# Expert stage of a graph and transformer block: tokens routed in two parts of 13 and 12 groups in place of three of 10, 9 and 6

## What is computed

```python
xn = _layernorm(x, axis=-1)
x = x + gnn(xn, edge_attr_64, src, dst, ...) + mix(xn, ...)   # edge attention; linear attention and MLP
x = x + ffn(_layernorm(x, axis=-1), ...)

# ffn: six experts of three 256x256 layers, two chosen per token
rh = relu(features @ router_w1 + router_b1)
expert_logits = softmax(rh @ router_w2 + router_b2)
top_w, top_i = top_k(expert_logits, 2)
routing_weights = softmax(top_w)
# h1, h2, expert_out of each expert; the two chosen outputs, weighted and added
```

## Time and profile before

| | |
|---|---|
| median of three runs | 2500.79 us |
| the profiled execution's own time | 2505.82 us |
| its span | 2504.1 us |
| TensorE busy | 1926.2 us (77%) |
| GpSimd busy | 1668.5 us (67%) |
| VectorE busy | 1556.8 us (62%) |
| ScalarE busy | 611.9 us (24%) |
| mean granted TensorE clock | 0.859 of full speed |

### The profile page before, as it was taken

How to read it: one execution, slowest core, us unless ns; L and a number is a source line. 1 busy time by engine, 2 the same in 40 slices (tenths; PEclk the granted TensorE clock), 3 DMA queues, 4 the chain that set the end, 5 groups by cost and what they waited for, 6 DMA issues and landing times.

```text
span 2504.1 us, 39252 instructions
## 1 busy us (share of the span) xinstructions
PE 1926.2 (77%) x11133; PEld 1530.7 (61%) x11133; DVE 1556.8 (62%) x3687; ACT 611.9 (24%) x2634; POOL 1668.5 (67%) x1278
## 2 busy tenths in 40 slices
PE   3899577659887777777878767878775778999992
PEld 1444476547766665665666656656654667888882
DVE  4778599877766565566566655656654883226263
ACT  1333388611111111111111111111101323433430
POOL 5554466688888888888888888888884277316164
PEclk8999756569988898898888888888887888999996
DMA  5766788534454444445544444455456455437363
GB/s 155 205 205 189 253 299 294 190 98 133 124 151 127 123 128 123 123 124 134 140 127 123 127 123 123 123 146 132 123 125 182 133 163 153 129 111 199 102 191 96
DMA packets 310586, 378.65 MB, mean 151 GB/s; under 512 B 119740, under 2 KB 263832, under 8 KB 307376
## 3 DMA queue, kind: packets, MB, share of 16 engines
q1 hardware_dynamic: 168932, 234.02, 30.1%
q0 software_dynamic: 141568, 143.66, 23.3%
HBM read 291.57 MB, written 84.76 MB: 150 GB/s over the span
## 4 chain that ended last, share of the span: by engine, by line
PE 34%; POOL 19%; DVE 9%; issue 8%; DMA 5%; ACT 2%; DVEq 2%; SPq 0%; ACTq 0%; POOLq 0%
PE bank L692 32%; POOL wexp L633 17%; DMA wexp<-xn_rows,a_src 4%; PE bank L1018 1%; POOL g_all L679 1%; DVEq L1508 1%; DVE work L1744 1%; DVE work L1749 1%; DVE st L1752 1%; DVE onehot L1668 1%; DVE acc L1680 1%; DVE acc L1766 1%; DVE work L1518 0%; DVE work L1526 0%; SPq L339 0%
## 5 line engine op out<-in xcount | busy, mean ns | idle before, releaser
L633 POOL DMA_INDIRECT wexp<-xn_rows,a_src x900 | 1126.8, 1252 | 274.0 <-issue 258.4
L692 PE MATMUL bank<-wexp,onehot 125*125 125x257 f32 x1800 | 548.7, 459 | 269.9 <-DMA wexp<-xn_rows,a_src 158.8
L692 PEld LDWEIGHTS bank<-wexp,onehot 125*125 125x125 f32 x1800 | 393.5, 228 | 404.2 <-issue 295.1
L1680 DVE TENSOR_TENSOR acc<-bank,acc 125x257 f32 x450 | 190.8, 424 | 419.9 <-PE bank L692 385.0
L1668 DVE TENSOR_SCALAR onehot<-iota_r,a_rel,a_hi 125x125 f32<-125x125 f32 x900 | 289.1, 389 | 0.0
L679 POOL DMA_INDIRECT g_all<-y_d,work x100 | 126.4, 1264 | 218.9 <-DMA y_d<-g_all 117.6
L692 PE MATMUL bank<-g_all 128*128 128x256 f32 x1040 | 238.0, 382 | 8.0 <-DVE g_all L1908 4.6
L692 PEld LDWEIGHTS bank<-g_all 128*128 128x128 f32 x1040 | 193.6, 191 | 33.8 <-issue 6.1
L692 PE MATMUL bank<-work,w_s 128*128 128x250 f32 x800 | 189.0, 378 | 27.9 <-ACT work L1155 27.1
L692 PE MATMUL bank<-s_p,wexp 128*128 128x49 bf16 (+1 forms) x3600 | 143.7, 203 | 62.4 <-DVE wexp L1473 60.6
L692 PEld LDWEIGHTS bank<-work,w_s 128*128 128x128 f32 x800 | 150.4, 191 | 55.7 <-ACT work L1155 35.3
(11 more groups left out here) (269 smaller groups left out, 2739.1 us busy)
## 6 DMA issues: line engine op xcount, KB each, us to landing
wexp<-lr_d SPq DMA_DIRECT2D x75, 750.0 KB
wexp<-in_attr SPq DMA_DIRECT2D x25, 896.0 KB
g_all<-sorted_d SPq DMA_DIRECT2D x65, 256.0 KB
y_d<-g_all SPq DMA_DIRECT2D x65, 256.0 KB, 3.0
wexp<-xn_rows,a_src POOLq DMA_INDIRECT x900, 3.9
sorted_d<-spare SPq DMA_DIRECT2D x48, 256.0 KB, 5.5
sorted_d<-spare SPq DMA_DIRECT2D x24, 384.0 KB, 4.6
work<-xn_rows SPq DMA_DIRECT2D x38, 224.0 KB
```

The lines of the kernel that those rows point to most:

```text
L633: pool.indirect_dma_start(ring[:, 2 * z + k, 0:D], None, xn_rows, bass.IndirectOffsetOnAxis(ap=a_src[:, n // CS, j:j + 1], axis=0)).then_i ...
L692: return pe.matmul(o, l, r, start=first, stop=last_, **kw)
L1680: v.tensor_tensor(to, bank[3 + z % 2][0:R, 0:D + 1], to, ALU.add).then_inc(s("summed"), 1)
```

## The change

`PARTS` becomes (13, 12). All that is sized by it follows: the tiles, the fills, the columns of the routing's tiles, and which groups have their residual on GpSimd. The scratch tiles of the routing (`r_pr`, `r_oh`, `r_m`) are wider now and move from `work` to `spare`, which the earlier stages no longer need by then.

```diff
--- before.py
+++ after.py
@@ -58,7 +58,7 @@
 EPS = 1e-5
 ROUND = 12582912.0
 T = 256
-PARTS = (10, 9, 6)
+PARTS = (13, 12)
 TILES = tuple((2 * GROUP * n + EXPERTS * (T - 1)) // T for n in PARTS)
 GROUP0 = tuple(sum(PARTS[:k]) for k in range(len(PARTS)))
 TILE0 = tuple(sum(TILES[:k]) for k in range(len(PARTS)))
@@ -238,9 +238,9 @@
         rt_i = per[:, 450:550].rearrange("p (b k) -> p b k", k=2).bitcast(I32)
         lg_b = per[:, 550:850].rearrange("p (b k) -> p b k", k=EXPERTS)
         te_i = per[0:1, 850:850 + ALL_TILES].bitcast(I32)
-        sp_ = work[0:R, 512 * 13:512 * 14]
-        r_pr, r_oh = sp_[:, 0:120], [sp_[:, 120:240], sp_[:, 240:360]]
-        r_m = sp_[:, 360:480]
+        r_w = EXPERTS * NB
+        r_pr, r_m = spare[0:R, 0:r_w], spare[0:R, 3 * D:3 * D + r_w]
+        r_oh = [spare[0:R, (1 + k) * r_w:(2 + k) * r_w] for k in range(2)]
         rx = sb("rx", [R, 8, NB])
         r_cum = sb("r_cum", [R, NB * EXPERTS])
         r_e = sb("r_e", [R, 4, EXPERTS])
```

## The result

The change makes the kernel slower by a little over one per cent. Four runs gave 2527.75 to 2532.67 us, median 2529.96, against a median of 2500.91 for four runs of the kernel before (2499.56 to 2501.46): ratio 1.0117, 95% interval 1.0100 to 1.0135, or +29 us. The forecast was +27.0 us, 2527.8, with a range of 2518 to 2535.

The account below looks back on a forecast made before the run. Bounds by stretch: GpSimd's gathers, VectorE's normalisation and routing, TensorE's tiles, then GpSimd alone. Entry 19.1, tiles -28.1, tail +36.4, gathers -0.4, fills 0 sum to +27.0 us on 2500.8: 2527.8 us, range 2518 to 2535.

Parts of the forecast that it names:

- Tiles: Expert tiles on TensorE: 60 in place of 65, five fewer at 5.62 us each, wholly on the path, -28.1 us.
- Tail: GpSimd's gathers behind the last tile: 48 in place of 24, at 1.515 us each, +36.4 us, bounds 36.3 to 38.1.
- Entry: Way into the first tile: later routing and 12 more sends delay the first load by 35.1 us, layer one by 19.1.
- the 16 us that were free: Before the first tile: about 16 us of the sends' lateness was free, as TensorE and VectorE were still finishing routing.
- The price of 1.0 us for each residual that moved to GpSimd: Normalisation before routing: residuals of groups 10 to 12 on GpSimd add 1.0 us each, +3.0; low end -0.7.
- Gathers beside tiles: Part 0's returning gathers beside part 1's tiles: first bundle's stall 4.3 us, second's 2.6 vanishes; net -0.4, ends -2.5 and +3.
- Fills: Zero fills in the edge loop: 6 units a turn in place of 7, hidden under gathers, 0 us; low end -5.
- Gathers that hold up the tiles: Rival on gathers returning beside tiles: 11 tiles each lengthened by 1.02 us, loss 11, total +34 us, 2535; chance 0.07.
- The cheaper entry: Rival before the first tile: GpSimd's residuals miss VectorE and landing takes 5.3; entry 12.2, total +20 us, 2521; chance 0.12.
- the edge loop gave nothing back: Rival in the edge loop: one fill transfer fewer returns up to 37 us, 2491, so not slower; chance 0.04.
- an edge loop that ends before 1886: Sign in the edge loop: the forecast is wrong if this loop ends earlier than 1886 us.
- the missing routing: Before TensorE's tiles: one routing of some 13 us fewer, said not to matter because VectorE and TensorE stand idle until rows come.

## Why the prediction was right

**Tiles, -28.1.** From first to last store -27.9, of which +0.2 are more stall: -28.1. Right.

**Tail, +36.4.** +37.3. The gathers are there in the number and in the unbroken row that was forecast; their mean is 1.525 us, not 1.515, and the first one comes 0.3 us later after the last store. Over five kernels, from the tail's first gather to the end: 31.0 us for 16 gathers, 42.8 for 24, 62.4 for 36, 79.8 for 48, 99.0 for 60. That is 68.0/44 = 1.545 us a gather.

**Entry, +19.1.** +18.6 at the first store, by its own steps: routing begins 16.2 us later (16.3 forecast), takes 15.1 in place of 14.0 us up to the first send (+1.1; 0.9 forecast), and the load comes +35.1 later, to the tenth what was forecast. Of the 16 us that were free, 16.5 were used up. That the steps agree to the tenth is luck: the run with more fills does the same work, and there routing begins 15.1 us later than before and the load comes 34.3 later. At the first layer of tile 0, where the forecast counted, the change is 19.7 later (2099.46 against 2086.18, each from VectorE's first instruction): the load took 4.42 us to land, where 3.5 had been taken, though the forecast's own terms give 2104.9 for its 2105.3. The first store is at +18.6 mainly because the eight matmuls of that layer took 2.42 us in place of 3.75. With a clock that stays low for longer, as in the run with more fills, it is +19.9. The forecast had allowed 2 us for just this in its high end.

One reading in it was wrong, and did no harm by luck. The send at 2055.76 was taken for the 40th; it is the 39th, and the last send of part 0 is at 2060.40, behind the pause. So the 8.5 us "from the last send to the first tile load" are 4.64 to the 40th send and 3.90 of landing. In the change the pause lies inside the row of 52 sends and the landing is 3.88. The price of a send was misread with it: 58.15 us are 38 distances, 1.53 each, not 39 at 1.491. The twelve sends more were at 1.49 all the same (17.7 us against 17.9), because the longer distances stand at the front of the row. Both ways make 35.1, since the forecast carried the pause along in either place. With parts that had changed the number of pauses it would have shown.

The price of 1.0 us for each residual that moved to GpSimd, from the pair's 1.74 against 0.74 us, gave the right value for the begin of routing: 16.3. The 12.6 that the forecast set against it belongs to the pitch of 4.21; VectorE's instruction count alone would have given 13.3 - 3 x 0.87 = 10.7. The four kernels that differ from another only by fewer residuals on GpSimd bear the direction out, at 0.6 to 1.1 us a group. The Trainium skill's page "SBUF — State Buffer", section "Who interferes with whom", says that VectorE in a two-port mode and GpSimd shut each other out for a whole instruction. The trace agrees in that the pair takes 1.74 us beside GpSimd and 0.74 alone, in the change as well; that the ports are the cause no run here tried apart.

**Gathers beside tiles, -0.4.** +0.2 (4.9 for 26 blocks, 4.3 forecast, against 4.7 before). Right within the bounds given.

**Fills, 0.** Right, by the run with seven units.

**The rivals.** None of them happened in the change. Gathers that hold up the tiles, given 0.07, did happen in the kernels with parts of 11, 10, 4. The cheaper entry would have needed GpSimd's residuals to miss VectorE; the edge loop gave nothing back. One sign that the text named as proof against it, an edge loop that ends before 1886, did appear (1881), and means nothing: the loop's end scatters by some 9 us from one execution to the next. A sign must be counted from the start of its own stage.

**What the forecast did not see** is that the missing routing is worth something by itself. It was called without effect here, which is right for 13 groups, where VectorE and TensorE stand idle (TensorE for 35.9 us before the first tile; the forecast had some 28). With 10 groups in the first part it gave 9.6 us.

What remains open: why the medians differ by 29.0 and the stages by 28.0, which is within the scatter (the run with more fills gives 29.8 by its stages); and the cause of GpSimd's pause.

## What to carry to other kernels

When work goes through a pipeline in parts, the first part's size is paid at the entry (here 11.4 us a group: 4.4 to 5.4 of normalisation and four sends, less what other work hides, 16.5 us in the change), the last part's size at the end (6.1 us a group of gathers), and a part fewer saves only the rounding (5 tiles, 28 us) and one fixed step that may be hidden. Large parts at both ends lose; the better split here had a small last part, as long as enough tiles remain behind the previous part's gathers to hide them. And count stage times from the first instruction of the stage: 9 us of scatter in an earlier loop are a third of what was to be explained.

## What the runs showed of the hardware that was not expected

GpSimd pauses after the 39th send of a part, in all eleven profiles: 4.62 to 4.79 us from that send to the next in place of 1.49. It comes again 39 sends into the second part where that has more than 39 (after the 91st send with 52 in part 0, the 79th with 40, the 83rd with 44), with 4.8 to 6.7 us, and not where the second part has 36. The gathers of the tail, up to 60 in a row, have no such pause. Its cause was not tried.

TensorE's clock at the first tile comes back after unlike times, though TensorE stood idle for some 35 us or more in each case: at a mean of 0.92 from 2.5 to 5.5 us after its first transpose in the change, still at 0.50, 1.2 GHz, after 4.6 us in the run with residuals on VectorE for groups 10 to 12. From first load to first store 20.0 and 19.8 us pass in two kernels (13, 12 and 16, 9) and 21.3, 22.2 and 22.3 in three others, though all five wait for the same thing. What decides between them was not tried.

Work taken off VectorE and given to GpSimd made VectorE slower: the residual costs it 0.87 us a group, and with GpSimd at work beside it the pair that writes `acc` takes 1.74 us in place of 0.74.
